# A four-layer transformer stack on one core: PSUM from three fixed rings to one pool of eight banks, and the filling products from a tile written on the chip

## The reference

```python
# L0: attention 0 on x (causal), attention 1 with ctx as keys and values, then fc1/fc2
lengths = jnp.sum(energy[:, :, 0, :] != 0, axis=-1)          # masks keys past the length
score = jax.nn.softmax(energy / jnp.sqrt(dk), axis=-1)
x1 = _layernorm(x + z); x2 = _layernorm(x1 + z); out = _layernorm(x2 + relu(x2@fc1)@fc2)
# L1: attention 2, both sides normed, x + out@Wo + bo, then silu MLP of width 512
# L2: attention 3 (causal, self), attention 4 (ctx), relu MLP of width 512, pre-norm, residuals
# L3: attentions 5, 6, 7 with relu on Q, K, V, 4 heads of 32 wide, a mask on absent keys,
#     each followed by enc = leaky_relu(enc @ Wff[i] + bff[i], 0.2) + enc
```

## Time and profile before

| | us |
|---|---|
| median of 3 runs | 1190.44 (1185.55 to 1195.29) |
| the profiled execution | 1186.32 |
| its span | 1184.4 |
| TensorE's mean granted clock in it | 0.974 of 2.4 GHz |
| PE busy | 1052.0 (89%) |
| DVE busy | 870.4 (73%) |
| ACT busy | 601.5 (51%) |
| POOL busy | 220.9 (19%) |

### The profile page before, as it was taken

How to read it: one execution, slowest core, us unless ns; L and a number is a source line. 1 busy time by engine, 2 the same in 40 slices (tenths; PEclk the granted TensorE clock), 3 DMA queues, 4 the chain that set the end, 5 groups by cost and what they waited for, 6 DMA issues and landing times.

```text
span 1184.4 us, 37373 instructions
## 1 busy us (share of the span) xinstructions
PE 1052.0 (89%) x16224; PEld 761.2 (64%) x16351; DVE 870.4 (73%) x2508; ACT 601.5 (51%) x857; POOL 220.9 (19%) x320
## 2 busy tenths in 40 slices
PE   6869987989998999998989798869999989999895
PEld 4647655657767766665666576647676667766564
DVE  3688799965566655788896879997755765588886
ACT  4335444556656545554544353536756654654552
POOL 4001113210100111222320000231010010123333
PEclk9899999989999999999999998989999999999998
DMA  6001000000000000000000000000000000000001
GB/s 235 2 11 29 3 2 2 2 2 2 2 2 3 2 11 19 10 2 1 11 1 11 20 2 2 2 1 2 2 3 2 3 2 2 2 1 1 1 2 36
DMA packets 13715, 13.52 MB, mean 11 GB/s; under 512 B 617, under 2 KB 13170, under 8 KB 13298
## 3 DMA queue, kind: packets, MB, share of 16 engines
q1 hardware_dynamic: 13554, 11.14, 3.0%
HBM read 9.04 MB, written 2.10 MB: 9 GB/s over the span
## 4 chain that ended last, share of the span: by engine, by line
PE 48%; DVE 38%; ACT 5%; POOL 4%; issue 4%; DMA 0%; SPq 0%; POOLq 0%; DVEq 0%; ACTq 0%
DVE mx L1257 9%; PE bank L857 9%; PE bank L665 9%; PE bank L889 9%; PE bank L732 5%; PE bank L863 5%; PE bank L652 4%; DVE stats L999 4%; DVE X L1023 4%; PE bank L765 3%; ACT PT L932 2%; DVE Y L1009 2%; DVE Y L1017 2%; DVE Y L1061 2%; DVE mv L1002 2%
## 5 line engine op out<-in xcount | busy, mean ns | idle before, releaser
L932 ACT ACTIVATE PT<-bank 128x1024 f32<-128x1024 f32 x184 | 185.0, 1025 | 220.6 <-PE bank L863 181.4
L1257 DVE TENSOR_REDUCE mx<-bank 128x16 f32<-128x1024 f32 x184 | 217.9, 1216 | 34.4 <-PE bank L863 25.9
L857 PE MATMUL bank<-KQ 32*128 32x128 f32 (+3 forms) x4416 | 194.8, 267 | 46.2 <-DVE mx L1257 16.9
L857 PEld LDWEIGHTS bank<-KQ 32*128 32x128 f32 (+3 forms) x4416 | 159.8, 161 | 108.7 <-DVE mx L1257 31.5
L889 PEld LDWEIGHTS bank<-V,PT 128*64 128x64 f32 x5888 | 185.7, 139 | 54.2 <-issue 37.7
L889 PE MATMUL bank<-V,PT 128*64 128x32 f32 (+2 forms) x5888 | 202.4, 225 | 8.4 <-DVE Y L1061 4.1
L665 PE MATMUL bank<-xf,W_all 128*128 128x512 f32 x336 | 180.0, 633 | 6.1 <-ACT xf L903 3.5
L1283 POOL TENSOR_SCALAR ve<-mv 128x4 f32<-128x4 f32 x64 | 15.6, 243 | 675.8 <-DVE mv L1002 662.7
L903 ACT ACTIVATE KQ<-bank,c 128x512 f32<-128x512 f32 x160 | 100.6, 687 | 69.5 <-PE bank L665 68.9
L903 ACT ACTIVATE V<-bank 64x512 f32<-64x512 f32 x128 | 79.2, 619 | 43.9 <-PE bank L765 42.0
L1052 DVE RECIPROCAL rd<-bank 128x32 f32<-128x32 f32 (+1 forms) x128 | 37.6, 294 | 73.2 <-PE bank L889 72.6
(11 more groups left out here) (112 smaller groups left out, 1593.3 us busy)
## 6 DMA issues: line engine op xcount, KB each, us to landing
W_all<-weights SPq DMA_DIRECT2D x1, 2880.0 KB, 12.4
...
```

The source lines that it names most:

```text
L857: last[u] = pe.matmul(banked[u // 2][:, at:at + 2 * S], stationary[rows_, seq].rearrange("p r t -> p (r t)"), moving[rows_, seq].rearrange ...
L932: act.activation(PT[:, n % NPT, :], banks.of("B", a, s, v)[:], ACT.Exp, scale=float((D // (2 * PAIRS[a])) ** -0.5)).then_inc(*banks.drain( ...
L1257: dve.tensor_reduce(dst, banks.of("A", a, s, v)[:].rearrange("p (u m t) -> p u m t", u=2, t=S), AX.X, ALU.max).then_inc(*banks.drain(("A", ...
```

## The change

There is one pool of eight banks, held as four tensors of two banks each. Each step of the PE table names its place behind an `@`: one digit per tile, a bank (0 to 7) for a tile of one bank, a pair (0 to 3) for a score tile, so that `A0@03` takes pairs 0 and 3, and `x@7` bank 7. A claim waits for the readers of each bank that it takes. All four tables of order are new too: of the 1072 PE steps 375 stand at the same place in the list as before, the median step is moved by one place, none by more than 17. The steps themselves, and with them all work but the filling products, are the same.

Of the 159 score steps of the 16-head attentions that follow another score step, 157 shared both their tiles with the score step ahead of them; in the new table 49 share both pairs, 88 share one, 22 none. The filling products read a new tile `warm` (128x128, all ones, broadcast four times) that GpSimd writes as its first instruction. There are 394 of them instead of 295, in 279 steps. By group and attention, before and after: 0.0 13 and 32, 0.1 38 and 32, 0.2 28 and 41, 0.3 12 and 14, 0.4 17 and 23, 0.5 14 and 35, 0.6 19 and 24, 0.7 18 and 20, 0.8 6 and 6; 1.0 24 and 24, 1.1 20 and 48, 1.2 31 and 45, 1.3 7 and 1, 1.4 8 and 5, 1.5 6 and 6, 1.6 19 and 16, 1.7 9 and 12, 1.8 6 and 10.

```diff
 ORDER = {
     "PE": """
-        0.0.0 x+1; 0.0.1 x; 0.0.2 x; 0.0.0 pq pk pv; 0.0.1 pq; 0.0.0 first; 0.0.1 pk; 0.0.0 length; 0.0.1 pv+1; 0.0.0
...
-        v1; 0.0.2 A1+1; 0.0.3 A0; 0.1.0 x1+2 kv pk+1; 0.0.2 maxrow; 0.0.3 A1; 0.0.1 v2+1; 0.0.2 B0; 0.0.1 v3; 0.0.3
...
+        0.0.0 x@7+6; 0.0.1 x@6; 0.0.2 x@7; 0.0.0 pq@5 pk@4; 0.0.1 pq@7; 0.0.0 pv@6 first@5; 0.0.1 pk@7; 0.0.0
...
+        v0@1+4 v1; 0.0.2 A1@12+3; 0.1.0 x1@7; 0.0.3 A0@03; 0.1.0 kv@3+1 pk@5+3; 0.0.2 maxrow@4; 0.0.3 A1@01; 0.0.1
...
-        self.filled = [ctx.enter_context(nc.semaphore(f"filled{k}")) for k in range(len(BANKS))]
-        self.tensor = [ctx.enter_context(nc.psum_tensor(f"bank{k}", [P, w], F32)) for k, w in enumerate(BANKS)]
-        self.section, self.uses, self.last, self.turn = section, [0] * len(BANKS), {}, {}
+        self.filled = [ctx.enter_context(nc.semaphore(f"filled{k}")) for k in range(8)]
+        self.pairs = [ctx.enter_context(nc.psum_tensor(f"pair{k}", [P, 1024], F32)) for k in range(4)]
+        self.section, self.uses, self.last = section, [0] * 8, {}
...
+    def view(self, k, width):
+
+        at = 512 * (k % 2)
+        return self.pairs[k // 2][:, at:at + 512 * width]
...
-    def claim(self, due, ring, *use):
-
-        n = self.turn[ring] = self.turn.get(ring, -1) + 1
-        k = ring[n % len(ring)]
-        if self.section.known and k in self.last:
-            for sem, count in self.section.known["readers"][self.last[k]].items():
-                due[sem] = max(due.get(sem, 0), count)
-        self.last[k] = use + (self.section.group,)
+    def claim(self, due, k, width, *use):
+
+        use += (self.section.group,)
+        for bank in range(k, k + width):
+            if self.section.known and bank in self.last:
+                for sem, count in self.section.known["readers"][self.last[bank]].items():
+                    due[sem] = max(due.get(sem, 0), count)
+            self.last[bank] = use
...
-BANKS = (1024, 1024, 512, 512, 512, 512)
 OUT, WIDE, FILL = 160, 32, 512
-RING_S = (0, 1)
-RING_O = (2,)
-RING_M = (3, 4, 5)
...
-                    loaded(c16_in)
-                    held[use], = banks.take(pe, ring, use)
+                    loaded(pool, "warm")
+                    held[use], = banks.take(pe, places[:1], width, use)
                     for _ in range(n):
-                        pe.matmul(held[use][:, 0:FILL], K16("identb"), c16[:, 0:FILL], start=True, stop=True)
...
+                        pe.matmul(held[use][:, 0:FILL], warm[:], warm[:].unsqueeze(1).broadcast_to((P, FILL // 128, 128)),
+                                  start=True, stop=True)
...
                     uses = [(kind, a, s, 2 * half + k) for k in range(2 if PAIRS[a] == 8 else 1)]
                     early = [held.pop(use) for use in uses if use in held]
-                    return early + banks.take(pe, RING_S, *uses[len(early):])
+                    return early + banks.take(pe, places[len(early):], 2, *uses[len(early):])
...
                 section.group = 0
+                g_.memset(warm[:], 1.0).then_inc(*pool.mark("warm"))
```

More of the change, by code:

```diff
@@ L58 @@
[L58 to L72, removed]
@@ new lines @@
+        ksum@6+1; 0.7.1 v0@5; 0.7.3 pq@4+1; 0.7.1 v1@7; 0.7.3 maskrow@6; 0.8.0 x1@5; 0.7.2 v0@3; 0.7.3 A0@0; 0.8.0
+        ff@2; 1.0.0 x@3; 0.7.2 v1@7+1; 1.0.0 pq@6 pk@5 pv@7+2; 0.7.3 pv@6 maxrow@5; 1.0.0 first@4+1; 0.7.3 B0@0+2;
+        1.0.0 length@7+1; 0.8.1 x1@6+1; 0.7.3 v0@7+2; 1.0.0 maskrow@6; 0.7.3 v1@5; 0.8.1 ff@4; 1.0.1 x@3+1 pq@7+2
+        pk@6; 1.0.0 A0@01; 0.8.2 x1@7+1; 1.0.1 pv@6; 0.8.2 ff@7+1; 1.0.1 first@5+1; 1.0.2 x@4; 1.0.0 A1@01; 1.0.2
+        pq@7; 1.0.1 length@5; 0.8.3 x1@4+1; 1.0.1 maskrow@7+1; 0.8.3 ff@5+2; 1.0.1 A0@01; 1.0.2 pk@7 pv@6; 1.0.3
@@ L273 @@
+        mx0 nm; 1.8.1 O0; 1.7.2 mrow; 1.8.1 O1; 1.8.0 n1; 1.8.1 sum; 1.7.3 km lrow; 1.8.1 n1; 1.7.3 mx0 nm mrow; 1.8.2
+        O0 O1 sum; 1.8.0 leaky; 1.8.3 O0; 1.8.2 n1; 1.8.3 O1 sum n1; 1.8.2 leaky; 1.8.1 leaky; 1.8.3 leaky
     """,
     "POOL": """
-        0.1.0 sum; 0.1.1 sum; 0.1.2 sum; 0.1.3 sum; 0.2.0 kvstats sum; 0.2.1 kvstats sum; 0.2.0 z n3; 0.2.2 kvstats;
-        0.3.0 wo; 0.2.1 z n3; 0.3.1 wo; 0.2.2 sum; 0.2.3 kvstats sum; 0.2.2 z n3; 0.2.3 z n3; 0.3.3 wo; 0.3.0 down
-        addff; 0.3.2 wo; 0.3.1 down addff; 0.3.2 down addff; 0.3.3 down addff; 0.4.0 addwo; 0.4.1 addwo; 0.4.2 addwo;
@@ L283 @@
[L283 to L287 removed]
+        0.1.0 sum; 0.1.1 sum; 0.1.2 sum; 0.1.3 sum; 0.2.0 kvstats sum; 0.2.1 kvstats sum; 0.2.0 z n3; 0.2.1 z; 0.3.0
@@ L288 @@
+        leaky; 1.7.1 sum; 1.7.0 leaky; 1.7.2 sum; 1.7.1 leaky; 1.7.2 leaky; 1.7.3 sum leaky; 1.8.0 sum; 1.8.1 sum;
+        1.8.2 sum; 1.8.3 sum; 1.8.0 leaky; 1.8.2 leaky; 1.8.1 leaky; 1.8.3 leaky
     """,
@@ L390, in take @@
         return taken
-    def claim(self, due, ring, *use):
-        n = self.turn[ring] = self.turn.get(ring, -1) + 1
-        k = ring[n % len(ring)]
-        if self.section.known and k in self.last:
-            for sem, count in self.section.known["readers"][self.last[k]].items():
-                due[sem] = max(due.get(sem, 0), count)
-        self.last[k] = use + (self.section.group,)
+    def claim(self, due, k, width, *use):
[5 more added lines that the diff above has]
+            self.last[bank] = use
         self.uses[k] += 1
-        self.section.counts["filled"][self.last[k]] = k, self.uses[k]
-        return self.tensor[k]
+        self.section.counts["filled"][use] = k, width, self.uses[k]
+        return self.view(k, width)
     def full(self, *use):
@@ L408, in of @@
     def of(self, *use):
-        return self.tensor[self.section.known["filled"][use + (self.section.group,)][0] if self.section.known else 0]
+        return self.view(*(self.section.known["filled"][use + (self.section.group,)][:2] if self.section.known else (0, 2)))
     def ready(self, *use, ago=0):
@@ L415, in ready @@
             return self.filled[0], 0
-        k, n = self.section.known["filled"][use + (self.section.group - ago,)]
+        k, _, n = self.section.known["filled"][use + (self.section.group - ago,)]
         return self.filled[k], n
@@ L529, in network @@
         expo = sb("expo", [P, 3, NT])
+        warm = sb("warm", [P, 128], BF16)
         section = Section(known)
```

487 lines of the change are left out of this document (258 added, 229 removed).

## The result

The changed kernel takes 1157.17 us (median of 4 runs, 1156.48 to 1158.6) where the kernel before, run beside it, took 1192.87 (4 runs, 1185.55 to 1195.46): a ratio of 0.9709, 95% interval 0.9671 to 0.9746. The profiled executions stand at 1156.84 and 1186.32 us. The forecast was 1178.7 us, 11.7 less than before; 29.5 us went by the profiled executions, 35.7 by the medians. The direction and the range (1155 to 1203) held, the size did not: three times the forecast.

A forecast was written before the change was run, and what follows sets the result against it. PE was taken to bind in attentions 2 to 4, DVE in attentions 0 and 1. Start -1.7, banks -8, filling products +4, clock -6 and order 0 gave -11.7 us from 1190.4: 1178.7 us, range 1155 to 1203.

The forecast's parts named there:

- the new order: All engines' lists: steps move by a median of one place, no work changes; put at 0, bounds -8.6 and +8.6 us.
- Banks, -8: PE's 37.6 us of waits for banks, mostly at score steps: 15.4 us go, half passes to the end, -8 us.
- Start, -1.7: Program start: PE no longer waits for constant `c16`, so the first projection starts 1.4 to 1.8 us earlier; taken as -1.7.
- Filling products, +4: 99 more filling products on PE, 20.5 us not free at the start; a fifth overruns idle gaps, +4 us.
- clock, -6: PE's lower clock, mainly passages out of attention 1: 20 of 61.6 us return to 2.4 GHz, saving 6 us.
- no wait of 2 us for `mx`: Sign in the new profile: no PE wait of 2 us for DVE's maxima at a score step.
- over 0.85 in both passages: Sign: granted clock over 0.85 in the 30 us holding each group's passage from attention 1 to 2.
- 30 us of DVE idle time: Sign: DVE idle time in attentions 0 and 1 falls from 39 us to about 30.
- rival 3: All of it: bank waits fall further (-30) and the clock stays up in both passages (-14); 1148.7 us, chance 15%.
- Rival 1: Banks don't bind: DVE limits attentions 0 and 1, bank waits reappear one step later; 1190.7 us, chance 17%.
- Rival 2: Added filling products overrun, all 20.5 us on the path, and banks gain nothing; 1209.2 us, chance 13%.
- the forecast's own case: The sum of the terms holds: range 1166 to 1192 us, chance 50%.

The follow-up runs named there:

- experiment 1: Changed kernel's code (one bank pool, warm tile) with the old lists and their 295 filling products: 1185.5 us, ratio 0.9957 to the kernel before.
- experiment 2: Changed kernel with the old list's number of filling products at each step (295): 1164.2 us, ratio 0.9753 to the kernel before.
- experiment 4: Changed kernel, new lists, without any filling product: 1157.0 us.
- experiment 5: Old lists with the eight banks in one pool, chosen bank places and no filling product: 1187.1 us.
- experiment 9: Changed kernel without filling products, with the four old lists and old-order banks only from about 225 to 310 us: 1165.7 us, ratio 0.9776 to the kernel before.
- experiment 3: Kernel before, rings and lists unchanged, its filling products reading the warm tile instead of the constant: 1191.4 us, ratio 0.9991.
- experiment 8: Changed kernel with filling products kept only in attentions 0 to 2 (222 of 394): 1150.6 us, ratio 0.9667 to the kernel before.
- experiment 12: Changed kernel with filling products only in attentions 0 to 2 and group 1's 6, 7 and last layer (260 of 394): 1150.2 us, ratio 0.9665.

## Why the prediction was wrong

- **The step that failed is the one on the new order, "What it does beside the terms above I put at 0", with bounds of 8.6 us either way.** The new lists with their bank places are worth 21.3 us with the old 295 filling products (experiments 1, 2) and 30.1 without any (4, 5). I had judged the term by distance, the median step one place on, and by a tenth of PE's 86.2 us of waits for operands. But on an engine that walks its list strictly, one place decides whether DVE has work in the 3.8 us of a `down` product (experiment 9): DVE's wait of 4.1 us puts off PE's next operand by 2.0 us, and the lower clock behind it costs more than the wait. I also looked at PE's waits alone: 38% of the chain was DVE's, whose waits for PE fell as well (for `rd` from 72.6 to 59.5 us, for `mx` from 25.9 to 18.5). How the rest of the gain divides between waits, clock and bank places is not shown; up to 7.4 us can be places (experiment 5).
- **Banks, -8:** near in size taken alone, -6.2 with the start included (-8.7 to -1.6 by the interval). By the way that I had reckoned, 15.4 us of waits gone and half of it passed on, the trace of experiment 1 has 11.7 gone at the score steps. The Trainium skill's "Adding PSUM double-buffering gave no further gain" (TensorE: Matmul & The Clock Gate, section "HAM oscillation — how this bites in real kernels") comes near: here it is 0.4%, with an interval that excludes 0. But the pool is also what lets these lists exist: with tiles in turn from the three rings, steps of the new lists wait for each other in a circle, by the waits of the program alone, so there is no such kernel to time. The gain of the lists thus needs the pool. Whether other lists, nearly as good, would run on the rings was not tried.
- **Start, -1.7:** the projection came at 10.72 us, inside 10.3 to 11, and PE's first instruction at 0.98. It was given back within the first 17 us: in experiment 3 (-0.3 us of median) by DVE, whose list waits for stream 3's input first, in the changed kernel by a later rise of the clock. Both have 0.2 us left at `first`. The step left out DVE's list and what the clock does between the turns.
- **Filling products, +4, and clock, -6:** as a sum -2. The fair measure is experiment 2 against the changed kernel, the same lists with 99 products fewer: -7.0 us, 5 by the ratios. The time at the lower level is 0.032 x 1161.9 / 0.5 = 74.4 us there and 0.025 x 1155.0 / 0.5 = 57.8 us in the changed kernel, 16.6 less, where I had 20. Against the kernel before, with its other lists, it hardly fell (61.6). The term named the passages out of attention 1; group 0's got the clock back, group 1's did not (0.77), and between 60 and 240 us it fell from 0.98 to 0.93, where DVE binds. The overrun is real in 351 to 545 us, 2.6 to 3.9 us by the traces of experiments 4, 8 and 12. All 394 products together are worth 0.2 us less than nothing, within the scatter.
- **What the new profile should have shown:** 394 loads, the start and the waits for `mx` and `PT` under 20 us (10.3) came true; no wait of 2 us for `mx` (4.7), a mean clock of 0.98, over 0.85 in both passages (1.00 and 0.77) and 30 us of DVE idle time in attentions 0 and 1 (36.0) did not.
- **Rivals:** the time, 1157.2, is nearest to rival 3's 1148.7, but by another mechanism: it had -30 for banks and -14 for the clock. Rival 1 (banks don't bind) is out on its own point by experiment 1's interval, if narrowly, and wrong on the sum, for it too had the order at nothing. Rival 2's overrun was found at 2.6 to 3.9 us, far from its 20.5, and was covered. That the measured time lies within 1155 to 1203 us is luck: the forecast's own case ended at 1166, and the lower end was set for rival 3's banks and clock, not for the order.
